# Writing a gather table in two transfers, one-hot tables from 16-bit numbers, and the last block's slots ahead of its masks

## What is computed

```
xn = _layernorm(x)
x  = x + attention(xn) + experts(xn)

probs = softmax(xn @ router_w.T)
w = _top_p_weights(probs, 0.9)
for e in range(8):
    y = (silu(xn @ gate_w[e].T) * (xn @ up_w[e].T)) @ down_w[e].T
    out = out + y * w[:, e:e + 1]
```

## Time and profile before

| | |
|---|---|
| time, median of 3 runs | 874.52 us (873.92 to 874.6) |
| the profiled execution, its own time | 880.18 us |
| its span | 878.5 us |
| its mean granted TensorE clock | 0.939 of full |
| PE, DVE, ACT, POOL busy (share of the span) | 89%, 60%, 44%, 37% |
| first stage, up to the first gathered tile on PE | 0 to 403 us |
| second stage | 403 us to the end |

### The profile page before, as it was taken

One profiled execution on the slowest core, in us unless ns is written; L12 is line 12 of the kernel. 1 busy time (PEld: TensorE's weight loads), 2 busy tenths in 40 slices (PEclk: granted clock), 3 DMA queues, 4 the chain that ended last, 5 costly groups with the idle time before them and its releaser, 6 DMA issues.

```text
span 878.5 us, 19529 instructions
## 1 busy us (share of the span) xinstructions
PE 784.6 (89%) x6592; PEld 699.6 (80%) x6593; DVE 526.8 (60%) x1170; ACT 389.5 (44%) x909; POOL 328.6 (37%) x366
## 2 busy tenths in 40 slices
PE   5889898989898989945999999999999999999993
PEld 4657676767676767635998999999989999999993
DVE  4567767677767776664456455464464554645642
ACT  3325252535343435333455454464454554644541
POOL 2001010101010101542565665665665655656663
PEclk9969898989899989776999999999999999999997
DMA  2120202020202020430535335353353353443332
GB/s 103 67 73 2 97 0 96 0 96 0 96 0 96 0 72 1 156 50 25 132 54 128 61 54 126 60 127 55 61 127 56 58 127 54 106 83 59 57 58 36
DMA packets 38561, 59.54 MB, mean 68 GB/s; under 512 B 4112, under 2 KB 33808, under 8 KB 37392
## 3 DMA queue, kind: packets, MB, share of 16 engines
q0 software_dynamic: 19776, 27.16, 19.0%
q1 hardware_dynamic: 18768, 32.16, 10.5%
HBM read 37.15 MB, written 22.15 MB: 68 GB/s over the span
## 4 chain that ended last, share of the span: by engine, by line
PE 58%; issue 13%; DVE 9%; DMA 9%; ACT 6%; POOL 4%; POOLq 1%; ACTq 0%; DVEq 0%; SPq 0%
PE A L1049 10%; PE A L1051 9%; PE A L1050 9%; DMA xg<-gather_table,g_idx 6%; PE O L1049 4%; PE O L1051 4%; PE O L1050 4%; PE S L1089 3%; PE A L1280 2%; PE S L1049 2%; PE S L1051 2%; PE S L1050 2%; DMA gather_table<-xna 2%; PE O L1116 2%; ACT xna L541 2%
## 5 line engine op out<-in xcount | busy, mean ns | idle before, releaser
L455 POOL DMA_INDIRECT out<-ybuf,s_idx x98 | 157.7, 1609 | 63.1 <-POOL s_idx L451 46.7
L1049 PE MATMUL A<-gT_hi,w_hi 128*128 128x256 f32 x588 | 167.1, 284 | 6.0 <-issue 4.5
L1050 PE MATMUL A<-gT_lo,w_hi 128*128 128x256 f32 x588 | 166.3, 283 | 0.0
L1051 PE MATMUL A<-gT_hi,w_lo 128*128 128x256 f32 x588 | 166.2, 283 | 0.0
L441 POOL DMA_INDIRECT xg<-gather_table,g_idx x100 | 102.5, 1025 | 113.1 <-ACT w_tok L656 67.5
L356 POOL TENSOR_TENSOR on_lo<-on,on_hi 128x512 fp32r<-128x512 f32 x16 | 20.9, 1305 | 328.7 <-ACT on_hi L511 328.7
L1023 DVE TENSOR_TENSOR h_lo<-h,h_hi 128x256 fp32r<-128x256 f32 x196 | 83.3, 425 | 59.6 <-ACT h_hi L684 59.6
L1049 PEld LDWEIGHTS A<-gT_hi,w_hi 128*128 128x128 f32 x588 | 111.8, 190 | 7.8 <-issue 7.8
L1049 PE MATMUL O<-w_hi,h_hi 128*128 128x256 f32 x392 | 115.4, 295 | 0.0
L1050 PEld LDWEIGHTS A<-gT_lo,w_hi 128*128 128x128 f32 x588 | 111.7, 190 | 0.0
L1051 PEld LDWEIGHTS A<-gT_hi,w_lo 128*128 128x128 f32 x588 | 111.6, 190 | 0.0
(11 more groups left out here) (182 smaller groups left out, 1645.9 us busy)
## 6 DMA issues: line engine op xcount, KB each, us to landing
w_raw<-wffn SPq DMA_DIRECT2D x9, 1536.0 KB, 7.0
gather_table<-xna SPq DMA_DIRECT2D x8, 528.0 KB, 3.0
xa<-x SPq DMA_DIRECT2D x8, 512.0 KB, 3.5
xr<-x SPq DMA_DIRECT2D x8, 512.0 KB, 4.9
out<-yout SPq DMA_DIRECT2D x8, 512.0 KB
out<-ybuf,s_idx POOLq DMA_INDIRECT x104, 3.9
xg<-gather_table,g_idx POOLq DMA_INDIRECT x100
w_raw<-wqk_nat SPq DMA_DIRECT2D x1, 512.0 KB, 5.0
```

The costliest lines, as they stand in the source:

```text
L455: pool.indirect_dma_start(out=out, out_offset=bass.IndirectOffsetOnAxis(ap=s_idx[:, sub:sub + 1], axis=0), in_=ybuf[:, sub, :], in_offset= ...
L1049: mm(out_ap, l_hi, r_hi, start=(k == 0), stop=False)
L1050: mm(out_ap, l_hi, r_lo, start=False, stop=False)
L1051: return mm(out_ap, l_lo, r_hi, start=False, stop=(k == n - 1))
```

## The change

The table is written in two transfers. `xna` holds the tokens alone, and goes out as soon as `norm_apply` is done (`tokens_out`); the weights go to a tile of their own, `wgt`, and out by a transfer of 32 bytes a row, with a semaphore `wtab_in` of its own. The wait in `norm_apply` names `table_in` as before, which now counts the token transfers. The slot numbers and the counting tables become 16-bit, the slot numbers are stored twice side by side, and the comparisons run over pairs; `one_hot` has two pieces instead of four. In the last block `slots` and the one-hot pieces come ahead of masks 6 and 7 on DVE, `one_hot_tokens` comes first in ACT's second half, and PE multiplies the slot tables before the last mean of squares. The last head normalization on DVE moves behind the index tables. The split of expert 0's weights moves behind everything else: its high parts follow `heads_hi` on ACT, and its low parts go from POOL to DVE, behind the residual. SP's order at the end stays.

```diff
-        lo_iota = sb("lo_iota", [P, P])
-        hi_iota = sb("hi_iota", [P, NT // P])
+        lo_iota = sb("lo_iota", [P, P], BF16)
+        hi_iota = sb("hi_iota", [P, NT // P], BF16)
...
-        xna = sb1("xna", [P, TT, AUG])
+        xna = sb1("xna", [P, TT, D])
+        wgt = sb1("wgt", [P, TT, NE])
...
+            def tokens_out(s):
+                sp.dma_start(table_blk[s][:, :, 0:D], xna[:, :, :]).then_inc(table_in, DMA)
+
             sp.wait_ge(xn_ok, 1)
+            tokens_out(0)
             sp.dma_start(xa[:, :, :], x_blk[1]).then_inc(x_in, DMA)
...
                 sp.wait_ge(w_ok, s + 1)
-                sp.dma_start(table_blk[s], xna[:, :, :]).then_inc(table_in, DMA)
+                sp.dma_start(table_blk[s][:, :, D:AUG], wgt[:, :, :]).then_inc(wtab_in, DMA)
                 if not first:
                     sp.wait_ge(y_ok, 2 * s + 2)
                     sp.dma_start(out_blk[s - 1], yout[:, :, :]).then_inc(yout_free, DMA)
+                if not last:
+                    sp.wait_ge(xn_ok, s + 2)
+                    tokens_out(s + 1)
                 if more:
-                    sp.wait_ge(xn_ok, s + 2)
                     sp.dma_start(xa[:, :, :], x_blk[s + 2]).then_inc(x_in, DMA)
...
                 if last:
-
-                    for piece in range(PIECES):
-                        pool.wait_ge(whi_ok, piece + 1)
-                        low_piece(0, piece * PW)
                     add_zeros(0)
...
                 if not last:
                     front(s + 1)
+                if last:
+                    one_hot_tokens(s)
                 head_rstd(s, 0)
...
             heads_hi(NBLK - 1, 1)
-            one_hot_tokens(NBLK - 1)
+            act.wait_ge(w_in, DMA)
+            for piece in range(PIECES):
+                high_piece(0, piece * PW)
...
                     if not first:
-                        dve.wait_ge(table_in, DMA * s)
-                    v.tensor_tensor(xna[:, :, D:AUG], pr[:, :, :], keep[:, :, :], ALU.mult).then_inc(w_ok, 1)
+                        dve.wait_ge(wtab_in, DMA * s)
+                    v.tensor_tensor(wgt[:, :, :], pr[:, :, :], keep[:, :, :], ALU.mult).then_inc(w_ok, 1)
...
-                chain.link(v.tensor_copy(slot_lo[:, :, :], lo_i[:, :, :]))
-                chain.link(v.tensor_tensor(slot_hi[:, :, :], slot[:, :, :], slot_lo[:, :, :], ALU.subtract))
+                twice = lambda a: a[:, :, :].rearrange("p t e -> p (t e)").unsqueeze(2).to_broadcast([P, TT * NE, 2])
+                chain.link(v.tensor_copy(slot_lo[:, :, :], twice(lo_i)))
+                chain.link(v.tensor_tensor(slot_hi[:, :, :], twice(slot), slot_lo[:, :, :], ALU.subtract))
+                one_hot_rows(oh_hi, hi_iota, slot_hi, slice(0, TT * NE)).then_inc(slot_ok, 1)
...
+            def one_hot_rows(table, numbers, slots2, rows):
+
+                n, m = rows.stop - rows.start, numbers.shape[1] // 2
+                return v.tensor_tensor(
+                    table[:, rows, :].rearrange("p n (m two) -> p n m two", two=2),
+                    numbers[:, :].rearrange("p (m two) -> p m two", two=2).unsqueeze(1).to_broadcast([P, n, m, 2]),
+                    slots2[:, rows, :].unsqueeze(2).to_broadcast([P, n, m, 2]), ALU.is_equal)
...
                 if not first:
-                    one_hot(s - 1, 2)
-                    one_hot(s - 1, 3)
+                    one_hot(s - 1, 1)
                     head_norm(s - 1, 1, chain)
...
                 if not first:
                     add_indices(s - 1)
+                if last:
+                    slots(s, 1, chain)
+                    one_hot(s, 0)
...
                 masked_scores(s, 6)
+                if last:
+                    one_hot(s, 1)
...
-                if last:
-                    slots(s, 1, chain)
-                    one_hot(s, 0)
-                    head_norm(s, 1, chain)
                 if not last:
                     queries(s + 1, 0)
-                one_hot(s, 1)
...
             second_half(NBLK - 1, True, chain)
-            one_hot(NBLK - 1, 2)
-            one_hot(NBLK - 1, 3)
             add_indices(NBLK - 1)
...
+            head_norm(NBLK - 1, 1, chain)
             for i in range(2):
                 add_residual(NBLK - 1, i)
+            for piece in range(PIECES):
+                first_low_piece(piece)
...
             second_half(NBLK - 1, True)
+            pe.wait_ge(idx_ok, NBLK)
+            slot_tokens(NBLK - 1)
             pe.wait_ge(ln_o_ok, 2 * NBLK - 1)
             mean_squares(NBLK - 1, 1)
             output_projection(NBLK - 1, 0)
-            pe.wait_ge(idx_ok, NBLK)
-            slot_tokens(NBLK - 1)
```

More of the change, by code:

```diff
@@ L195, in build @@
         slot = sb1("slot", [P, TT, NE])
-        slot_lo = sb1("slot_lo", [P, TT, NE])
-        slot_hi = sb1("slot_hi", [P, TT, NE])
+        slot_lo = sb1("slot_lo", [P, TT * NE, 2], BF16)
+        slot_hi = sb1("slot_hi", [P, TT * NE, 2], BF16)
         oh_lo = sb1("oh_lo", [P, TT * NE, P], BF16)
-        oh_hi = sb1("oh_hi", [P, TT * NE, NT // P])
+        oh_hi = sb1("oh_hi", [P, TT * NE, NT // P], BF16)
         oh_rhs = sb1("oh_rhs", [P, TT * NE, 2, NT // P], BF16)
@@ L220, in build @@
         w_tok = sb2("w_tok", [P, (NE * MAX_TILES + 1) * SUB * NE])
+        w_hi.append(sb2("w_hi1", [P, WE], F32R))
+        w_lo.append(sb2("w_lo1", [P, WE], F32R))
         A = [ps(f"A{i}", [P, 512]) for i in range(4)]
@@ L274, in _, with first_half @@
             sp.dma_start(w_raw[:, :], wffn[0]).then_inc(w_in, DMA)
+            def tokens_out(s):
+                sp.dma_start(table_blk[s][:, :, 0:D], xna[:, :, :]).then_inc(table_in, DMA)
             sp.wait_ge(xn_ok, 1)
+            tokens_out(0)
             sp.dma_start(xa[:, :, :], x_blk[1]).then_inc(x_in, DMA)
-            def first_half(s, first, more):
+            def first_half(s, first, more, last=False):
                 if not first:
@@ L300, in _ @@
             first_half(NBLK - 2, False, False)
-            first_half(NBLK - 1, False, False)
+            first_half(NBLK - 1, False, False, True)
             sp.wait_ge(y_ok, 2 * NBLK)
@@ L422, in _ @@
             pool.wait_ge(table_in, DMA * NBLK)
+            pool.wait_ge(wtab_in, DMA * NBLK)
             done = pool.alloc_register("tiles_done")
@@ L540, in norm_apply @@
                 for t in range(TT):
-                    last = a.activation(xna[:, t, 0:D], xa[:, t, :], ACT.Identity, bias=nmr_x[:, t:t + 1],
+                    last = a.activation(xna[:, t, :], xa[:, t, :], ACT.Identity, bias=nmr_x[:, t:t + 1],
                                         scale=rstd_x[:, t:t + 1])
@@ L597, in first_half @@
                     norm_apply(s + 1)
-                if last:
-                    act.wait_ge(w_in, DMA)
-                    for piece in range(PIECES):
-                        high_piece(0, piece * PW)
                 keys_by_token(s, 1)
@@ L813, in slots, with one_hot @@
                 chain.link(v.tensor_scalar(lo_i[:, :, :], slot_i[:, :, :], P - 1, None, ALU.bitwise_and))
-                chain.link(v.tensor_copy(slot_lo[:, :, :], lo_i[:, :, :]))
-                chain.link(v.tensor_tensor(slot_hi[:, :, :], slot[:, :, :], slot_lo[:, :, :], ALU.subtract))
[L816 to L819, removed]
+                twice = lambda a: a[:, :, :].rearrange("p t e -> p (t e)").unsqueeze(2).to_broadcast([P, TT * NE, 2])
+                chain.link(v.tensor_copy(slot_lo[:, :, :], twice(lo_i)))
+                chain.link(v.tensor_tensor(slot_hi[:, :, :], twice(slot), slot_lo[:, :, :], ALU.subtract))
+                one_hot_rows(oh_hi, hi_iota, slot_hi, slice(0, TT * NE)).then_inc(slot_ok, 1)
                 v.tensor_scalar(from_end[:, :], from_end[:, :], float(-BLK), None, ALU.add)
                 chain.link(v.tensor_copy(base[:, 0, :], base[:, TT, :]))
[L823 to L827, removed]
+            def one_hot_rows(table, numbers, slots2, rows):
[4 more added lines that the diff above has]
+                    slots2[:, rows, :].unsqueeze(2).to_broadcast([P, n, m, 2]), ALU.is_equal)
+            def one_hot(s, part):
+                n = TT * NE // 2
+                ins = one_hot_rows(oh_lo, lo_iota, slot_lo, slice(part * n, part * n + n))
+                if part == 1:
                     ins.then_inc(lo_ok, 1)
@@ L855, in add_indices, with first_low_piece @@
                 v.tensor_scalar(tile_no[:, :], tile_no[:, :], float(TT), None, ALU.add)
+            def first_low_piece(piece):
+                dve.wait_ge(whi_ok, piece + 1)
+                cols = slice(piece * PW, (piece + 1) * PW)
+                v.tensor_tensor(w_lo[0][:, cols], w_raw[:, cols], w_hi[0][:, cols].bitcast(F32),
+                                ALU.subtract).then_inc(wsplit, 1)
             def first_half(s, first, last, chain):
@@ L965, in _ @@
             dve.wait_ge(table_in, DMA * NBLK)
+            dve.wait_ge(wtab_in, DMA * NBLK)
```

7 lines of the change are left out of this document (2 added, 5 removed).

## The result

| | before | after |
|---|---|---|
| median of 4 runs | 874.56 us (873.92 to 874.67) | 840.3 us (837.19 to 843.56) |
| ratio, 95% interval | | 0.961 (0.9573 to 0.9647) |
| profiled execution, its span | 880.18, 878.5 us | 840.22, 838.5 us |
| mean granted TensorE clock | 0.939 | 0.968 |
| DVE busy | 526.8 us | 495.9 us |

The kernel is 34.3 us faster. The profiled executions part by 36.0 us up to the first gathered tile, and by 4.0 us more behind it; the profile of before was 5.7 us above its median and that of after is at its median.

A forecast was written before the change was run, and what follows sets the result against it. First-stage blocks were taken as bound by PE's wait for `k_tok` and the slow-clock stretch behind it. Blocks -37.0 us, tail +2.5, sum -34.5, from the median 874.52 to 840.0 us; 8-in-10 range 832 to 854.

The forecast's parts named there:

- Part 1, the wait: Blocks 0 to 6: PE's wait of 3.37 us for ACT's `k_tok` at `state(s, 1)` goes, 23.6 us in all.
- Part 1, what is late next: From `state(s, 1)` to the first `project`, DVE sets the pace: 7.63 us instead of 9.40; blocks 39.3 us apart.
- The clock: After the `k_tok` wait the granted clock stands at 0.50; without that wait it is back at full.
- Part 2, the pace: 16-bit tables on DVE: high table 0.68 us instead of 1.22, half a low table of 2048 numbers 1.2 us.
- the old pace: Rival, chance 0.08: the 16-bit tables gain no speed; 4 us less gain in the blocks, 2 in the last: 846 us.
- Part 3: Last block reordered: computing gains, but the output queues behind 1536 KB of weights and lands 2.5 us later than before.
- The small transfer: Table weights in 512 pieces of 32 bytes on SP's queue: costed at nothing; slower only in a rival, chance 0.02.
- The slow tables: Rival, chance 0.08: DVE's 16-bit tables keep their pace, 846 us.
- the free tail: Rival, chance 0.10: the last output isn't held by the weights, or PE stays at full clock there: 834 us.
- a clock that stays low behind `state`: Rival, chance 0.12: clock doesn't recover after the index product, only the wait goes: 853.4 us.
- The second stage: From 403 us: carried over whole, as the change touches no instruction there apart from the rows it gathers.

The follow-up runs named there:

- part 1 alone: The kernel before with only the table's tokens and weights sent in two transfers; tables, last block and weight split as before: 848.16 us, ratio 0.9684.
- e8_old_last_block: The changed kernel with the last block back in its old order, POOL splitting expert 0's weights beside it: 835.74 us, ratio 0.9548.

## Why the prediction was right

**Part 1, the wait: right.** Seven waits of 3.37 us are gone, and part 1 alone is worth 28.5 us. Of the 1.77 us that the stretch was to get shorter, 0.8 came with part 1 alone and the rest with the shorter tables.

**Part 1, what is late next: right.** The walk gave 7.63 us for the stretch; 7.57 to 7.59 were measured in blocks 1 to 5, with PE waiting 0.67 us for mask 6. The period was to be 39.3 and is 39.24. Block 0 and the last stretch were a little shorter than assumed (6.75 and 7.38). From before to after, the last block's first projection moved from 329.71 to 291.56, by 38.15 us; the sum had 37.0.

**The clock: right in the changed kernel, too simple as a rule.** The stretch ran at 1.00. But the fall isn't a fixed surcharge on a wait. After 1.6 us the profiled execution shows none, after 2.8 us stretches lie anywhere from 7.5 to 10.9 us, and after 3.2 to 3.5 us, in the profile of before, the clock fell each time (0.56 to 0.80 over the stretch). A gain on PE's path that stands behind such a wait can't be added up from durations; taking the wait away is what makes the rest countable.

**Part 2, the pace: right.** 0.69 us for the high table against 0.68 taken, 1.22 against 1.2 for half the low one. But what part 2 is worth depends on part 1. With it, part 2 and part 3 together bring some 8 us (848.16 to 840), and part 2 without part 3 brings 12 (848.16 to 835.74), but some 5 us of each lie in the second stage, whose tiles were moved in the same kernels. Without part 1, part 2 brings nothing that can be measured. The term for the old pace was too small: the prediction gave it 4 us in the blocks and 2 in the last one (846), and with the old pace it measured 854.07. Where the tables are slow, the last block suffers by 5.6 us and not by 2, and the clock falls now and then (a period of 41.9 instead of 40.3).

**Part 3: right, and for the reason given.** The tail was to be 2.5 us longer and is 2.1. The waits came at their places: PE 2.45 us for mask 6 (2.6 expected) with the clock down to 0.66 in that slice, on its way back to full when the slot product ran; the eight low pieces 3.83 us (3.9); the output released 8.6 us after the weights' issue (7.8). Measured against the same kernel with the old last block, part 3 costs 4.9 us and not 2.1: the 2.8 between are that the old order, too, is shorter once part 1 is in (a tail of 70.8, and of 70.3 with part 1 alone, instead of 73.55). I had compared with the trace of before only. There the clock of the last block was 0.66 from 360 to 375 us, against 0.89 in the same 15 us of the old order with part 1 in. From the product of the ranks to the last product of the masked scores with the values are 14.16 us before (361.06 to 375.22), 11.05 in `e8_old_last_block` (321.95 to 333.00), and 11.12 with part 1 alone and the old tables, so these 3 us come with part 1 and its clock and not with the tables.

**The small transfer: right.** 512 pieces of 32 bytes landed in 1.8 us each time, sooner than the 3.0 of the full rows. The transfers beside it take longer (`xa` 6.1 us at the median instead of 3.5), and nobody waits for them.

**The rivals.** The slow tables and the free tail are each seen in an experiment and not in the changed kernel; a clock that stays low behind `state` although the wait is gone was seen in no run.

**The second stage: wrong, and the size of the sum partly luck.** The prediction carried the second stage over whole, since no instruction of it changed; it got 4.0 us shorter, with the tiles that were moved in SBUF. Up to the first gathered tile the sum was 34.5 and the profiles part by 36.0 (1.2 more from the blocks, 0.4 less delay in the tail). But the sum came from a profile that was 5.7 us above its median, and the second stage varies little between profiles of like kernels (475.2 to 476.8), so those 5.7 us most likely lie in the first stage. Of the 34.3 us between the medians some 30 then belong to the first stage (an estimate: 34.3 less the 4.0) and not 34.5. The forecast of 840.0 was met so closely because, by this estimate, two errors of about 4 us cancel.

## What to carry to other kernels

When one tile carries two things that are ready at different times, the transfer of the early one waits for the late one, and so does whoever writes the tile next; the price is that wait and, as after the waits of 3.2 to 3.5 us here, a low clock behind it. Follow a step that is moved through every queue that counts on it: here eight small subtractions, moved behind the residual, put 1536 KB ahead of the one transfer that the next stage waited for. The move cost 4.9 us, and two lines of SP's order gave 8 back. Ask of each wait which instruction really needs it: the gather didn't need the output, but started at once it ran into the weights, and only a start ahead of them paid. Measure the stage that you count as unchanged as well: here it hid 4 us.

## What the hardware showed that I had not expected

- Behind the same wait of 2.8 us, in one execution, the stretch took 7.5 us at a granted clock of 1.00 and 10.9 us at 0.58. The same kernel in another execution had none of the short ones.
- A comparison of 2-byte numbers in which one operand has a step of 0 along the row ran at the 32-bit pace (2048 numbers in 2.28 us); with the number stored twice and read in pairs it took 1.22 us.
- A gather of 256 rows, for which POOL otherwise waits 2.0 us, kept it waiting 5.1 us when 1536 KB of weights were issued 1.2 us ahead of it on another queue, 6.5 with 512 KB of output in flight as well, and 2.1 when the weights had been issued 4.7 us ahead. With the 512 KB of output alone it was 3.05.
- With `w_hi1` and `w_lo1` in another place of SBUF, the middle tiles of the experts that use them took mostly 8.73 us instead of 9.01, at a granted clock of 1.00 in both; that the place is the cause wasn't tested alone.
